# Weight loads and clearing moved into POOL's own program, and five rearrangements of a wide attention

## What is computed

```python
x = x + rwkv(ln(x))                      # layer 0
x = x + banded_attention(ln(x), ctx)     # "xattn0": 8 heads, projections, band, gate by ctx
x = x + ternary_mlp(ln(x))               # "ffn0"
x = x + causal_attention(ln(x))          # "attn1": 16 heads
x = x + plain_attention(ln(x), ctx, ctx) # "xattn1": 8 heads, no projections
x = x + top2_of_8_experts(ln(x))         # "moe"
```

```python
scores = einsum('bqhd,bkhd->bhqk', q, k) / sqrt(d)
scores = where(abs(i - j) <= 64, scores, -huge)      # xattn0 alone
o = einsum('bhqk,bkhd->bqhd', softmax(scores), v)
```

## Time and profile before

| | us |
|---|---|
| median of 3 runs (2756.8 to 2758.96) | 2758.41 |
| the profiled execution, its time | 2778.94 |
| its span | 2776.9 |

### The profile page before, as it was taken

How to read it: one execution, slowest core, us unless ns; L and a number is a source line. 1 busy time by engine, 2 the same in 40 slices (tenths; PEclk the granted TensorE clock), 3 DMA queues, 4 the chain that set the end, 5 groups by cost and what they waited for, 6 DMA issues and landing times. The chain is left out here.

```text
span 2776.9 us, 55137 instructions
## 1 busy us (share of the span) xinstructions
PE 2217.8 (80%) x19084; PEld 1573.4 (57%) x19084; DVE 1868.5 (67%) x5654; ACT 1154.9 (42%) x2616; POOL 892.0 (32%) x1488
## 2 busy tenths in 40 slices
PE   4787739999989982999959999388888888378796
PEld 3676626666666652999947777144444444245453
DVE  4999967787878767555526666478788786334245
ACT  1222215555555542222216666066666665132232
POOL 3565532222222214666630000232222221324422
PEclk9888859999999995999979999599999999589898
DMA  3000033333333310000030000533333331123434
GB/s 110 1 0 1 1 98 90 95 87 94 86 94 84 94 37 0 2 2 2 2 149 1 2 2 2 142 101 102 101 101 101 101 102 49 44 65 94 135 107 157
DMA packets 252306, 183.16 MB, mean 66 GB/s; under 512 B 29056, under 2 KB 246304, under 8 KB 251264
## 3 DMA queue, kind: packets, MB, share of 16 engines
q1 hardware_dynamic: 240416, 156.52, 20.4%
q0 software_dynamic: 7456, 18.92, 1.9%
q10 hardware_dynamic: 4160, 4.19, 0.5%
HBM read 94.47 MB, written 83.51 MB: 64 GB/s over the span
## 5 line engine op out<-in xcount | busy, mean ns | idle before, releaser
L764 ACT ACTIVATE xattn_pr<-ps 128x384 f32<-128x384 f32 (+1 forms) x1024 | 544.3, 542 | 459.6 <-PE ps L499 260.0
L483 PE MATMUL ps<-xattn_kp,xattn_qp 96*128 96x192 bf16 (+1 forms) x2048 | 375.0, 265 | 99.1 <-DVE xattn_mx L634 38.3
L496 PE MATMUL ps<-xattn_qp,xattn_kp 128*128 128x192 bf16 (+1 forms) x2048 | 412.0, 263 | 3.3 <-ACT xattn_pr L764 2.7
L634 DVE TENSOR_REDUCE xattn_mx<-ps 128x2 f32<-128x512 f32 x512 | 333.5, 678 | 119.7 <-PE ps L483 117.7
L514 PE MATMUL ps<-xattn_pr,xattn_vs 128*32 128x256 f32 (+1 forms) x4096 | 307.2, 372 | 35.1 <-ACT xattn_o L769 34.9
L630 DVE CUSTOM_DVE_ANT_0 xattn_masked<-ps,xattn_band 128x192 bf16<-128x192 f32 x1024 | 324.2, 354 | 13.2 <-issue 5.7
L496 PEld LDWEIGHTS ps<-xattn_qp,xattn_kp 128*128 128x128 bf16 x2048 | 178.7, 97 | 171.7 <-issue 91.1
L483 PEld LDWEIGHTS ps<-xattn_kp,xattn_qp 96*128 96x128 bf16 x2048 | 175.5, 99 | 176.7 <-DVE xattn_mx L630 60.6
L499 PE MATMUL ps<-xattn_band,xattn_ident 128*128 128x192 bf16 x1024 | 211.2, 247 | 0.0
L1002 PE MATMUL ps<-ffn_parts,gate_up_t 128*128 128x128 bf16 x3072 | 194.7, 220 | 2.1 <-DVE ffn_parts L1120 2.1
L1002 PEld LDWEIGHTS ps<-ffn_parts,gate_up_t 128*128 128x128 bf16 x3072 | 184.5, 99 | 16.4 <-DVE ffn_parts L1120 2.5
(11 more groups left out here) (304 smaller groups left out, 4548.6 us busy)
## 6 DMA issues: line engine op xcount, KB each, us to landing
xattn_rows<-xattn_parts SPq DMA_DIRECT2D x128, 192.0 KB, 2.1
xattn_qp<-xattn_rows SPq DMA_DIRECT2D x256, 96.0 KB, 2.8
xattn_kp<-xattn_rows SPq DMA_DIRECT2D x256, 96.0 KB, 3.1
xattn_rows<-xattn_parts SPq DMA_DIRECT2D x128, 128.0 KB, 2.1
moe_rows_in<-region_zero SPq DMA_DIRECT2D x6, 1677.0 KB, 7.4
moe_xb<-moe_rows_in SPq DMA_DIRECT2D x78, 129.0 KB
xattn_rows<-xattn_parts SPq DMA_DIRECT2D x128, 64.0 KB, 1.8
moe_row<-moe_rows_out SPq DMA_DIRECT2D x16, 512.0 KB, 8.4
```

The lines of the kernel that those rows point to most:

```text
L483: mm = nc.tensor.matmul(ps[:, BANK_S + j % RING, mt * D:mt * D + width], qp[u][s][0:R_MAX, h, mt * P:(mt + 1) * P], kp[u][s][0:R_MAX, h, l ...
L496: mm = nc.tensor.matmul(out, kp[u][s][:, h, nt * P:(nt + 1) * P], qp[u][s][:, h, lo:lo + width], start=True, stop=not banded)
L634: ins = nc.vector.tensor_reduce(mx[s][:, h * NT:(h + 1) * NT], ps[:, BANK_S + j % RING, :].rearrange("p (m n) -> p m n", m=NT), AX.X, ALU.max)
L764: nc.scalar.activation(out, src, ACT.Exp, scale=HD ** -0.5).then_inc(exped, 1)
```

## The change

- `begin_loads` is gone. The transfers of weights are issued by POOL inside the wide attention, one at the end of each step from p = 2 on.
- `clear_regions` is gone. In attn1 POOL makes the zeros in step 2 and issues two of the six writes in each of steps 5, 9 and 13.
- `kp` and `qp` are not preset. The products use 99 rows in place of 128 (96 plus the three of the maxima), and the three rows of -1 come from a small tile `minus_one`, copied into each `kp` by four transfers that POOL issues at the stage's start; SP waits for neither.
- ACT copies the output (`keep_o`) ahead of the exponentials of turn 2, not behind them.
- `align` is in two: the sums at turn 4, the numerators at turn 5 (behind the multiply). `reciprocal_sums` move to turns 7 and 8, `normal_o` to 9, `gate_product` (xattn0) and `new_x` (xattn1) to 11.
- xattn1 uses a third score bank (bank 7, which only xattn0 needs for other things); PE may be three heads ahead of the maxima.
- In xattn0, for odd heads, PE adds the band to the scores by two more products, and DVE takes the maxima by one `tensor_reduce` (as in xattn1, over 2 x 192); even heads stay as they were.

```diff
-def begin_loads(core, name, loads):
...
-            for to, of in loads:
-                sp.dma_start(to, of).then_inc(landed, 16)
...
-    BANK_S, BANK_T, BANK_O, BANK_N, BANK_PREP, BANK_END = 0, 2, 4, 5, 6, 7
+    BANK_T, BANK_O, BANK_N, BANK_PREP, BANK_END = 2, 4, 5, 6, 7
     TURNS = 2 * QUADS
+    ALIGNED = 4, 5
+
+    SCORES = (0, 1) if banded else (0, 1, BANK_END)
...
+    R_MAX = ROWS * HD
+    R_ALL = R_MAX + PARTS
...
+    LATER_FROM = 2
+    later_loads, later_landed = later if later else ((), None)
...
+        def masked_by_product(h):
+
+            return h % 2 == 1
...
-                sp.wait_ge(preset, 1)
-                sp.wait_ge(k_preset, 1)
...
-                    wait(pe, maxed, idx(p, j) - RING + 1)
+                    wait(pe, maxed, idx(p, j) - len(SCORES) + 1)
...
+                        out = ps[:, SCORES[idx(p, j) % len(SCORES)], mt * D:mt * D + width]
+                        by_product = banded and masked_by_product(h)
+                        mm = nc.tensor.matmul(out, qp[u][s][0:R_MAX, h, mt * P:(mt + 1) * P],
+                                              kp[u][s][0:R_MAX, h, lo:lo + width], start=True, stop=not by_product)
+                        if by_product:
+                            mm = nc.tensor.matmul(out, ident16[:], band16[:, mt, :], start=False, stop=True)
...
-                        mm = nc.tensor.matmul(out, kp[u][s][:, h, nt * P:(nt + 1) * P], qp[u][s][:, h, lo:lo + width],
+                        mm = nc.tensor.matmul(out, kp[u][s][0:R_ALL, h, nt * P:(nt + 1) * P], qp[u][s][0:R_ALL, h, lo:lo + width],
...
-                        if j == 4 and not first:
-                            align(p - 1)
+                        if j in ALIGNED and not first:
+                            for half in range(2):
+                                align(p - 1, 2 * ALIGNED.index(j) + half)
...
-                        if banded and not first and j == 10:
+                        if banded and not first and j == 11:
                             gate_product(p - 1)
...
-                    if banded:
+                    if banded and not masked_by_product(h):
                         wait(v, maxed, idx(p, j))
...
+                        of = ps[:, bank, :].rearrange("p (m n) -> p m n", m=NT)[:, :, 0:width]
+                        ins = nc.vector.tensor_reduce(mx[s][:, h * NT:(h + 1) * NT], of, AX.X, ALU.max)
...
-                        if j in (6, 7) and not first:
-                            reciprocal_sums(p - 1, j - 6)
-                        if j == 8 and not first:
+                        if j in (7, 8) and not first:
+                            reciprocal_sums(p - 1, j - 7)
+                        if j == 9 and not first:
                             normal_o(p - 1)
-                        if j == 10 and not first and not banded:
+                        if j == 11 and not first and not banded:
                             new_x(p - 1, 1 - u)
...
-                for u in range(2):
-                    for s in range(S2):
-                        ins = nc.vector.memset(qp[u][s][:].rearrange("p h d -> p (h d)"), 0.0)
...
+                        if j == 2 and not first:
+                            keep_o(p - 1)
                         ahead = next_head(p, u, j + RING)
                         if there(ahead[0]):
                             exponentials(ahead[0], ahead[2])
                         if j == 0:
                             keep_maxima(p, u, 1)
-                        if j == 2 and not first:
-                            keep_o(p - 1)
...
                         fin.reciprocal_std(nc, g, p - 1)
+                    if 0 <= p - LATER_FROM < len(later_loads):
+                        to, of = later_loads[p - LATER_FROM]
+                        g.dma_start(to, of).then_inc(later_landed, 16)
+                nc.gpsimd.memset(minus_one[:].rearrange("p h d -> p (h d)"), -1.0).then_inc(minus_made, 1)
+                g.wait_ge(minus_made, 1)
                 for u in range(2):
                     for s in range(S2):
-                        ins = nc.gpsimd.memset(kp[u][s][:].rearrange("p h d -> p (h d)"), -1.0)
-                ins.then_inc(k_preset, 1)
+                        g.dma_start(kp[u][s][R_MAX:R_MAX + PARTS, :, :], minus_one[:]).then_inc(k_preset, 16)
...
-def clear_regions(core, ctx):
...
+    def clear(self, nc, g, q):
+        wait(g, self.cleared, 16 * PARTS_R * q)
...
+        for h in range(PARTS_R):
+            to = self.x_in[h][q * P * CLEAR:(q + 1) * P * CLEAR, :].rearrange("(p a) d -> p a d", a=CLEAR)
+            g.dma_start(to, self.zero[:]).then_inc(self.cleared, 16)
...
+                    if p == 2:
+                        regions.zeros(nc, g)
+                    if p >= 5 and (p - 5) % 4 == 0 and (p - 5) // 4 < regions.parts:
+                        regions.clear(nc, g, (p - 5) // 4)
                 over(g, PAIRS, step)
                 fin.reciprocal_std(nc, g, PAIRS - 1)
+                regions.all_cleared(g)
```

More of the change, by code:

```diff
@@ L610, in _ @@
                 multiply(PAIRS - 1, 1, TURNS - 1)
-                align(PAIRS - 1)
+                for quarter in range(4):
+                    align(PAIRS - 1, quarter)
                 if banded:
@@ new lines, with __init__, zeros, all_cleared @@
+class Regions:
+    def __init__(self, core, ctx):
+        nc = core.nc
+        self.core = core
+        self.x_in = [nc.dram_tensor(f"moe_rows_in{h}", (ROWS, ROW), F32).ap() for h in range(PARTS_R)]
+        self.y_out = [nc.dram_tensor(f"moe_rows_out{h}", (2 * REGION + ROWS, D), F32).ap() for h in range(PARTS_R)]
+        self.zero = core.sb("region_zero", [P, CLEAR, ROW], ctx=ctx)
+        self.made, self.cleared = core.sem("region_zero_made"), core.sem("region_cleared")
+        self.parts = ROWS // (P * CLEAR)
+    def zeros(self, nc, g):
+        nc.gpsimd.memset(self.zero[:].rearrange("p a d -> p (a d)"), 0.0).then_inc(self.made, 1)
+    def clear(self, nc, g, q):
+        wait(g, self.cleared, 16 * PARTS_R * q)
+        g.wait_ge(self.made, q + 1)
+        spare = self.core.c[:, C_SPARE + q * CLEAR:C_SPARE + (q + 1) * CLEAR]
+        nc.gpsimd.tensor_copy(self.zero[:, :, D:D + 1], spare.rearrange("p (a b) -> p a b", b=1)).then_inc(self.made, 1)
+        g.wait_ge(self.made, q + 2)
+        for h in range(PARTS_R):
+            to = self.x_in[h][q * P * CLEAR:(q + 1) * P * CLEAR, :].rearrange("(p a) d -> p a d", a=CLEAR)
+            g.dma_start(to, self.zero[:]).then_inc(self.cleared, 16)
+    def all_cleared(self, g):
+        g.wait_ge(self.cleared, 16 * PARTS_R * self.parts)
@@ L2544, in decoder @@
             rows, loads = load_ternary(core, own, i['L0_ffn_w_gate_up'], i['L0_ffn_w_proj'])
-            landed = begin_loads(core, "ternary_landed", loads)
-            wide_attention(core, "xattn0", i['ctx_2048'], wide)
+            landed = nc.alloc_semaphore(name="ternary_landed")
+            wide_attention(core, "xattn0", i['ctx_2048'], wide, later=(loads, landed))
             core.end_stage()
-            gu, pj = ternary_weights(core, own, rows, landed)
+            gu, pj = ternary_weights(core, own, rows, (landed, 16 * len(loads)))
             gated_mlp(core, "ffn0", FF // 256, lambda j, kt, ft: gu[:, kt, (2 * j + ft) * P:(2 * j + ft + 1) * P],
@@ L2566, in decoder @@
             experts, loads = load_experts(core, own, *(i[f'L1_ffn_W{n}'] for n in 'rgud'))
-            landed = begin_loads(core, "experts_landed", loads)
-            wide_attention(core, "xattn1", i['ctx_2048'])
+            landed = nc.alloc_semaphore(name="experts_landed")
+            wide_attention(core, "xattn1", i['ctx_2048'], later=(loads, landed))
             core.end_stage()
-            routed_experts(core, "moe", experts, regions, out, landed, rwkv)
+            routed_experts(core, "moe", experts, regions, out, (landed, 16 * len(loads)), rwkv)
 def kernel(**inputs):
```

80 lines of the change are left out of this document (25 added, 55 removed).

## The result

The changed kernel takes 3652.8 us (median of 4 runs, 3636.1 to 3658.6) where the one before takes 2758.05 us on the same chip: 1.3235 times as long (95% interval 1.3190 to 1.3279). The forecast was 2657, with a range of 2618 to 2702. It was wrong by 996 us, and in sign.

The account below looks back on a forecast made before the run. PE was taken as the fullest engine, DVE close behind, with waits for maxima and copies. Terms -24.1 - 18.4 - 5.5 - 2 - 44 - 10 + 3 = -101 off 2758.4 gave 2657 us, range 2618 to 2702.

Parts of the forecast that it names:

- the part on presets: Start of xattn0: ternary loads moved to POOL and presets dropped save 3.6 and 1.95 us, together 5.5.
- the rivals: Whole kernel: loops give nothing, 2709 us (with crowding 0.15); PE never waits, 2592 (0.08); slower, POOL held by loads (0.03).
- the slower one, POOL held by its loads: Wide attentions: an expert load holds POOL 7.7 us, PE waits for turned maxima, six loads cost 21 us; slower overall, 0.03.
- Clearing: Between ffn0 and attn1: with the zeros made and written inside attn1, that stage begins 24.1 us earlier.
- Expert loads and the start of xattn1: Start of xattn1: without the expert loads ahead of it the context lands sooner, saving 18.4 us, bounds 12.6 and 20.
- Start of xattn0: Start of xattn0: 3.6 us from six loads gone and 1.95 from POOL being free of clearing, together 5.5.
- Loads issued by POOL: Loops of the wide attentions: thirteen issues by POOL, below 1 us each, cost 3 us with zeros and crowding.
- Start of the loops: First 19 maxima of both wide attentions: faster odd heads and a third bank save perhaps 0.05 us each, 2 in all.
- Copy ahead: Both loops: PE's wait for the output copy goes to zero, 0.65 us per pair in xattn0 and 0.75 in xattn1.
- Third bank and order in xattn1: Loop of xattn1: together they relieve 0.68 us per pair of PE's wait for maxima, bounds 0 and 1.72.
- xattn0 with the band by products: Loop of xattn0: +1.33 us products, -1.0 relieved maxima, -0.65 copy; -0.3 per pair, -10 us in all.

Follow-up runs that it names:

- e1: The changed kernel with the row counts of the kernel before (scores 96, transposed scores 128) and the presets they need put back; 2660.6 us, 0.9645 of before.
- e4: e1 without the band by products, so no head of xattn0 takes it; 2642.1 us, 0.9576 of before.
- e11: The kernel before with only the clearing and the weights' loads moved into POOL's program, presets kept; 2722.2 us, 0.9875 of before.
- e7: e4 with ACT's copy of the output behind the exponential again; 2676.9 us, 0.9702 of before.
- e8: e4 with two score banks in xattn1 instead of three; 2658.9 us, 0.9644 of before.
- e10: e4 with the old turns of alignment, reciprocals, normal_o, gate product and new x; 2661.7 us, 0.9648 of before.
- e3: e1 with the scores alone cut to 48 rows, the transposed scores kept at 128; 2829.8 us, 1.0258 of before.

## Why the prediction was wrong

**The step that failed** is the part on presets. It priced what the change takes away (clearing) and never the products that are left: a term for 64 products of fewer rows per pair (32 of scores over 48 rows, 32 of transposed scores over 51) is missing, because I did not work the constant out. The runs put 992 us in its place. Had I done so, the nearest rows (96 and 128 rows at the same pace) would have said nothing for it; but that no row of a loop had a product under 96 rows was the reason to bound it from both sides, and the sum had no such bound. None of the rivals was near: for the slower one, POOL held by its loads, the runs show 3 us at most.

**What stands in its place**, for a pair of xattn0, as an estimate from the starts. Of the changed kernel's starts in one pair 92 come 0.27 us after the one before, where twice 0.0835 would be 0.167. e1's period less the 0.38 by which one start is late is 18.6, at half the clock 37.2. Eight groups of fp32 multiplies take 0.80 us each where e1 takes 0.463, so they do not quite double: 8 x (2 x 0.463 - 0.80) = 1.0 less. The changes add 92 x 0.103 = 9.5, nearly as much each as at the full clock. Together 45.7, and 45.21 measured. So of the 26.2 us a pair over e1 about 9 are changes and about 17 the clock. In xattn1, where four products in a row have few rows, a pair has only 8 changes beside those at the multiplies, and the clock moves between 0.5 and 1.0 (0.74 on the mean), the split was not made; 31 x (21.15 - 15.95) = 161 of the stage's 173 us are in the loop.

**The rest of the prediction**, point by point. e1 has everything but the rows and what hangs on them, and 2660.6 stands against 2657. That they are so close is partly luck: the pairs of xattn0 gained 9 us more than forecast, those of xattn1 5 less, and 5 us that the forecast took for the missing presets are not in e1.

*Clearing*: forecast 24.1. Of the changed kernel, in order of time:

```profile
2210.40 0.55 POOL L200 TENSOR_TENSOR x_stat<-ffn_rs,const_sb 128x1 f32<-128x1 f32 x1
2212.16 0.23 DVE L2495 CAST attn_ident<-const_sb 128x128 bf16<-128x128 f32 x1 [2.11 <-PEq L160]
```

The gap fell from 25.8 to 1.8: 24.0.

*Expert loads and the start of xattn1*: forecast 18.4.

```profile
2527.31 0.81 SPq L410 DMA_DIRECT2D xattn_qk<-in_ctx  x2
2527.31 1.79 POOL L874 MEMSET xattn_minus_one<- 3x2048 bf16 x1 [1.69 <-POOLq L160]
...
2529.40 0.63 ACT L793 ACTIVATE xattn_parts<-xattn_qk 128x512 bf16<-128x512 f32 x1 [8.40 <-DMA xattn_qk<-in_ctx]
2529.41 2.06 POOL L878 DMA_DIRECT2D xattn_kp<-xattn_minus_one  x4 [0.30 <-POOL xattn_minus_one L874]
...
2531.49 1.17 POOL L845 TENSOR_TENSOR xattn_rest<-xattn_qk,xattn_parts 128x512 f32<-128x512 f32 x1
```

The first rest starts 4.2 us into the stage; before, ACT's rounding ended 1776.98 + 0.63 - 1754.98 = 22.6 in the earlier trace rows, and the rest followed at once. That is 18.4. (The prediction's own terms, 1777.6 less 1759.4, give 18.2.) The context landed sooner than I took it to (2.1 us, not 3.3), and POOL's own four transfers became what the rest waits for, as forecast. In e1 and e4, with presets, the rest starts 7.4 us in, so 3.2 us of the 18.4 belong to the presets.

*Start of xattn0*: forecast 5.5.

```profile
369.62 1.79 POOL L874 MEMSET xattn_minus_one<- 3x2048 bf16 x1 [1.13 <-POOLq L160]
369.66 2.22 DVE L170 TENSOR_SCALAR xattn_xn<-x_now,x_stat 128x256 f32<-128x256 f32 x2 [2.22 <-PEq L160]
...
375.31 1.15 POOL L845 TENSOR_TENSOR xattn_rest<-xattn_qk,xattn_parts 128x512 f32<-128x512 f32 x1 [1.43 <-ACT xattn_parts L793]
```

375.31 - 369.62 = 5.7 against 380.64 - 369.45 = 11.2: 5.5. The two norms took 2.22 together with one clearing beside them, not 3.79: one of them waited, the other took its 0.4. This is the rule of the Trainium skill that the prediction weighed (SBUF — State Buffer, "Who interferes with whom"), and the trace agrees.

*Loads issued by POOL*: forecast under 1 us each, 3 us in all. Three of the six groups of that line in the changed kernel (the other five issues took 0.82 to 0.96):

```profile
L873 POOL DMA_DIRECT2D tern_rows<-in_L_ffn_w_gate_up x4: 817/831/872, 537.5 to 672.9; - x4
L873 POOL DMA_DIRECT2D tern_rows<-in_L_ffn_w_proj x2: 611/620/628, 718.5 to 764.2; - x2
L873 POOL DMA_DIRECT2D expert_gu<-in_L_ffn_Wg x2: 963/970/976, 2650.3 to 2719.2; - x2
```

At most 0.98 us, where the slower rival wanted 7.7. e11's periods are 0.06 and 0.03 above those of before, 2.8 us over 31 pairs. e11 as a whole gains 36 us; its boundaries sum to 24.0 + 15.2 + 3.6 = 43, less 3 for the loads. In the traces its moe stage does begin 39.9 us sooner (2319.5 against 2359.4); the 4 us lie behind that or between executions, and their cause is open.

*Start of the loops*: forecast 2. From the first rest to the fourth output copy e1 takes 1.9 us less than before in xattn0 and 6.6 less in xattn1; three shorter pairs are 1.8 and 3.8 of it, which leaves 2.9.

*Copy ahead*: forecast 0.65 and 0.75 per pair, measured 0.56 and 0.49 (e7). The mechanism held; the size was 0.26 too large in xattn1. e7's waits of 0.49 a pair in xattn0 plus 0.16 would be 0.65, and 0.56 came back. *Third bank and order in xattn1*: forecast 0.68 for both; the bank gave 0.44 (e8), the order -0.10 (e10). All of xattn1 came to 17.22 - 15.95 = 1.27 against 1.43. The three parts, each taken away alone, sum to 0.83 and not to 1.27, so 0.44 is covered by more than one of them; what the order gives without the third bank no run shows.

*xattn0 with the band by products*: forecast -0.3 per pair, measured 18.98 - 19.58 = -0.60. But the parts were not as I had them. The order alone is worth 0.69 there (e10), for which the sum had only the turn of the gate product, and the band by products costs 0.59 (e1 against e4). Its price of 1.33 us of products stands against a relief of 0.74, where I had 1.0: once the order has taken the late starts from 1.65 to 0.91 us a pair, there is less left to relieve. The two serve the same wait. (The late starts fall by 0.52 from e4 to e1; the other 0.2 of the relief I can't place, and the band by products was not run with the old order.) DVE's odd heads took 0.546 in e1, as forecast:

```profile
L646 DVE TENSOR_REDUCE xattn_mx<-ps 128x2 f32<-128x384 f32 x149 | 81.4, 546 | 51.9 <-PE ps L490 51.9
```

The fastest version that computes everything is e4: the change with the old row counts and presets and without the band by products, 2642.1 us. What stays open is why products over 48 and 51 rows hold the clock down. The runs show that they do so with few changes and with PE not idle, and that 48 rows beside 128 (e3) do not. Nor do they always: in the changed kernel's xattn1 the clock stood at 1.00 from 2800 to 2900 and at 0.53 in the 50 us behind it, with the same products.

## What to carry to other kernels

Work out every constant that a diff replaces, and read the shapes in the new code before the order: a product over fewer rows is no cheaper, and rows that are padded with zeros cost nothing while they keep the shapes alike. When an operation changes in a way for which the trace has no row, it is not free until a bound says so. When PE is busy all the time and nobody is waited for, read the granted clock and the times from start to start: the busy share hides both faults. Of parts that relieve the same wait, count the relief once, and take first the one that costs nothing (an order) before the one that adds work.
